# Spreading the next batch's first scans: the pace table of a two-stream recurrent kernel

## The reference, cut to what matters

```
x : (16, 512, 128)
xn = layernorm(x)
s  = selective_scan(xn, forward) + reverse(selective_scan(reverse(xn), backward))   # 2 x 16 states
g  = mixture_ffn(xn)          # router top-2 factor * (gelu(xn w1 + b1) w2 + b2)
x  = x + s * silu(g)                                   # "block A"
xn = layernorm(x)
s  = mamba2_like(xn)          # conv of 4 taps, chunked state recurrence, gated norm
g  = 2 layers of [ local attention over windows of 64 (8 heads of 64) ; gated ffn 128 -> 341 -> 128 ]
x  = x + s * silu(g)                                   # "block B"

selective_scan(x):  delta = softplus(low_rank(x));  h_t = exp(delta_t A) h_{t-1} + delta_t B_t x_t
                    y_t = sum over 16 states of C_t h_t + D x_t
```

## Time and profile before

| | |
|---|---|
| median of 3 runs | 4148.99 us (4142.99 to 4150.77) |
| profiled execution | 4157.49 us, span 4155.7 us |
| PE busy | 3285.2 us, 79% |
| ACT busy | 2603.5 us, 63% |
| DVE busy | 2552.8 us, 61% |
| POOL busy | 1726.6 us, 42% |
| mean granted TensorE clock | 0.905 of full speed |
| chain that ended last | PE 45%, DVE 20%, ACT 13%, issue 12%, POOL 9% |
| DMA engines | mean 5 GB/s, all but idle after the first slice |

### The profile page before, as it was taken

The page is one execution under the profiler, slowest core; times in us unless marked ns, Lnnn a source line. Parts: engine busy times, 40 slices in busy tenths (PEclk is TensorE's granted clock), DMA queues, the critical chain, the costliest instruction groups (busy, mean ns, idle before and its releaser), DMA issues.

```text
span 4155.7 us, 57708 instructions
## 1 busy us (share of the span) xinstructions
PE 3285.2 (79%) x17248; PEld 1929.7 (46%) x17248; DVE 2552.8 (61%) x4239; ACT 2603.5 (63%) x5871; POOL 1726.6 (42%) x1428
## 2 busy tenths in 40 slices
PE   4688878877788878887887788787887887888787
PEld 2354444544444444444544445445444544455443
DVE  5575766657556565666647666575666656666443
ACT  4466667665676656667666676656767566676554
POOL 2353343524435353343533535344353533535332
PEclk9798999999999999998989999989999899989898
DMA  2000000000000000000000000000000000000000
GB/s 83 3 1 1 6 1 6 1 1 7 1 7 1 1 7 1 7 1 1 6 1 7 1 7 1 1 7 1 7 1 1 7 1 7 1 1 3 1 3 3
DMA packets 18444, 21.03 MB, mean 5 GB/s; under 512 B 769, under 2 KB 17153, under 8 KB 17793
## 3 DMA queue, kind: packets, MB, share of 16 engines
q1 hardware_dynamic: 18048, 16.44, 1.2%
HBM read 12.24 MB, written 4.19 MB: 4 GB/s over the span
## 4 chain that ended last, share of the span: by engine, by line
PE 45%; DVE 20%; ACT 13%; issue 12%; POOL 9%; DMA 0%; DVEq 0%; POOLq 0%; ACTq 0%; SPq 0%
PE bank L564 8%; PE bank L626 5%; POOL hc L1464 4%; PE bank L813 3%; DVE tmp L1375 3%; DVE hst L1235 3%; PE bank L797 3%; PE bank L746 3%; POOL Pm L1537 2%; PE bank L547 2%; PE bank L532 2%; PE bank L773 2%; DVE tmp L1370 2%; DVE bank L1227 2%; PE bank L756 2%
## 5 line engine op out<-in xcount | busy, mean ns | idle before, releaser
L1464 POOL TENSOR_TENSOR hc<-hst,Cs 128x512 f32<-128x512 f32 x512 | 655.4, 1280 | 967.5 <-DVE hst L1235 957.2
L1235 DVE TENSOR_TENSOR_SCAN hst<-dA,bank 128x512 f32<-128x512 f32 x512 | 625.0, 1221 | 133.5 <-issue 58.9
L564 PE MATMUL bank<-W,xs 128*128 128x512 f32 x960 | 493.7, 660 | 25.5 <-DVE tmp L1375 23.8
L1537 POOL TENSOR_TENSOR Pm<-Pm,rinv 128x512 f32<-128x512 f32 x256 | 271.5, 1060 | 455.8 <-DVE rinv L1395 438.5
L927 ACT COPY Cs<-bank 128x512 f32<-128x512 f32 x512 | 299.3, 585 | 247.2 <-PE bank L547 217.4
L1227 DVE TENSOR_TENSOR bank<-u,bank 128x512 f32<-128x512 f32 x512 | 351.3, 686 | 158.7 <-PE bank L547 154.6
L547 PE MATMUL bank<-parts,sel 96*128 96x512 bf16 x1024 | 356.9, 423 | 107.8 <-DVE hst L1235 42.0
L1522 POOL TENSOR_TENSOR oT<-tmp 128x512 f32<-128x512 f32 x256 | 325.0, 1269 | 247.0 <-DVE tmp L1375 184.3
L921 ACT ACTIVATE dA<-delta,neg_a 128x512 f32<-128x512 f32 x512 | 372.6, 728 | 67.8 <-DVE hst L1235 67.1
L532 PE MATMUL bank<-C,hc 128*128 128x128 f32 x2048 | 353.6, 302 | 35.5 <-POOL hc L1464 35.5
L1054 ACT ACTIVATE Pm<-bank,mx 128x128 f32<-128x128 f32 x1024 | 366.7, 387 | 16.3 <-DVE mx L1389 14.7
(11 more groups left out here) (224 smaller groups left out, 6197.0 us busy)
## 6 DMA issues: line engine op xcount, KB each, us to landing
W<-wpack SPq DMA_DIRECT2D x1, 4498.0 KB, 13.3
x_tok<-x SPq DMA_DIRECT2D x16, 256.0 KB, 2.9
out<-xa SPq DMA_DIRECT2D x16, 256.0 KB, 2.2
rot<-tables SPq DMA_DIRECT2D x2, 512.0 KB, 15.9
wc_f<-taps SPq DMA_DIRECT2D x1, 1024.0 KB, 19.2
C<-cpack SPq DMA_DIRECT2D x1, 721.0 KB, 14.5
Pm<-mask SPq DMA_DIRECT2D x1, 320.0 KB, 14.8
tmp<-rowpack SPq DMA_DIRECT2D x1, 256.0 KB, 17.1
```

Of the source, the lines that this page charges most:

```text
L564: mm(b[:, :], weights, rhs, start=True, stop=True).then_inc(full(ring, job), 1)
L1235: v.tensor_tensor_scan(o, a, b, 0.0, ALU.mult, ALU.add).then_inc(sem("a_h"), 1)
L1464: g_.tensor_tensor(hc[:, k % 2, :], hst[:, k % 2, :], Cs[:, k % 2, :], ALU.mult)\
L1537: g_.tensor_tensor(windows, windows, over(rinv[:, k % 2, :], P), ALU.mult).then_inc(sem("t_P"), 1)
```

## The change

The table's entry that let P8 end with layer 1's fifteenth slot (B slot 46) is moved to B slot 42. The prologue's nine A slots are so run over the seven B slots from 35 on, for eleven before, and the ten scan slots are interpolated from B slot 42 to the last, for from B slot 46.

```diff
-PACE = [(0, 1), (LAYER, 10), (LAYER + UNITS_END, A_END), (LAYER + LAYER_SLOTS, HEAD + 5), (LAYER + LAYER_SLOTS + 4, PRO),
-        (LAYER + LAYER_SLOTS + UNITS_END, SCAN1), (B_SLOTS, A_SLOTS)]
+PACE = [(0, 1), (LAYER, 10), (LAYER + UNITS_END, A_END), (LAYER + LAYER_SLOTS, HEAD + 5), (LAYER + LAYER_SLOTS + 4, PRO), (LAYER + LAYER_SLOTS + 11, SCAN1),
+        (B_SLOTS, A_SLOTS)]
```

## The result

The changed kernel takes 4176.3 us (median of 4 runs, 4174.9 to 4182.8) against 4149.3 us for the kernel before on the same chip (4143.0 to 4150.8): ratio 1.0073, 95% interval 1.0057 to 1.0090. It is 27 us slower; 17 were predicted. The profiled execution has a span of 4181.0 us at a mean granted clock of 0.897 (before: 4155.7 us, 0.905).

What follows compares the result with a forecast made beforehand. No engine is busy over four fifths of the span, so the fit of five in-order queues was taken as the bound. 6.6 - 0.5 - 4.9 = +1.2 us a step, 14 steps, +17 us: 4166 us, range 4110 to 4205.

Steps and rivals of the forecast that it cites:

- Tail, -4.9: From the last feed-forward matmul to the next step's first: two DVE scans fewer, 4.9 us gained, bounds 3.8 and 5.6.
- the Silu and x2 pair: ACT's Silu and DVE's two x2 operations in the tail: if they set it, it stays above 12 us.
- Attention part, +6.6: Layer 1's first attention unit to its output projection: 5.8 us more on ACT plus 0.8 on PE, bounds 3.5 and 9.5.
- The two waits that the replay named: Behind DVE's delta block: PE waits about 3 us for POOL's Pm of unit 5, ACT 1.4 us at the gate.
- The gate block: P8's Silu table load, gate and load back on ACT, now ahead of the projection: 3.2 us.
- Three scans ahead of the projection: Two scans of 1.3 us on ACT before the last copies, and scan 2 on PE, some 0.8 us.
- The order of the prologue with the delta block: P0 to P4 earlier fill idle time; waits at the gate and first Gelu give it back: left out of the sum.
- Feed-forward, -0.5: From layer 1's projection to its last feed-forward matmul: one scan in slot 48 for two, 0.5 us gained, bounds 0 and 1.3.
- PE sets the pace: Rival, slots 38 to 42: PE never waits for the delta block, attention part grows only 3.5 us; 4122 us, chance 0.30.
- Half clock: Rival, attention part: matmuls behind PE's holes run at 1.2 GHz, 3 us more a step; 4208 us, chance 0.12.
- the holes it named: Two PE waits in the replayed attention part, 2183.3 to 86.5 and 87.8 to 91.0; half clock was expected behind the second.
- The two ends cancel: Rival: the tail gives what the attention part takes, within 0.5 us; 4149 us, chance 0.16.

Runs made afterwards that it cites:

- e1: Changed kernel's compressed prologue (B slots 35 to 41), with the ten scans left where the kernel before has them (slots 46 to 52): 4203.9 us, 1.0133.
- e7: e1 with the gate's Silu and its table loads on ACT moved to B slot 46, behind the attention part: 4170.4 us, 1.0058.
- e3: Changed kernel with the gate's Silu and its two table loads on ACT moved from slot 41 to 46, behind the last oT copy: 4112.7 us, 0.9911.
- e5: Changed kernel with 13 and 10 matmuls that nobody reads ahead of the transposes of layer 1's units 5 and 6: 4178.0 us, 1.0077.
- e8: Changed kernel with 6 and 6 unread matmuls on PE in the tail, ahead of scans 8 and 9: 4156.3 us, 1.0012.
- e11: Kernel before with the same 6 and 6 unread matmuls in the tail as e8: 4150.8 us, 1.0004.
- e6: e3 with DVE's delta block also cut in two around unit 6's maximum, unit 5's reciprocal and fo: 4167.0 us, 1.0045.
- e9: e3 with P0 to P8 one each in slots 35 to 43 and the ten scans over slots 44 to 52: 4149.5 us, 0.9996.
- e12: e10 with 8 more unread matmuls ahead of layer 0's transpose of unit 7: 4103.1 us, 0.9889.
- e10: e3 with the 6 and 6 unread matmuls in the tail of e8: 4090.1 us, 0.9856.

## Why the prediction was right, and where it was short

Direction, mechanism and the cancellation of two large terms were right: 81 us lost in the attention part, 65 won in the tail over fourteen steps (92 and 69 predicted). The 10 us by which the sum missed are a net figure, and that it is so small is in part luck. The attention part took 11 us less than forecast, the tail gave 3 less, and the feed-forward and the stretch behind the tail took 10 and 11 more; inside the attention part three wrong prices came out within 0.7 us a step of their sum. By its own steps:

- *Tail, -4.9.* -4.9 measured over the loop steps (13.5 predicted from L821's end to L1308, 13.6 measured). Scans on DVE set it, and the Silu and x2 pair did not take their place.
- *Attention part, +6.6.* +5.9 by the table's cuts, 5.7 from the first score matmul to L797. The two waits that the replay named came out within 0.1 us, their places didn't: the delta block starts 28.0 us behind the first score matmul (30.4 predicted), the transpose of unit 5 38.4 (41.0), L797 50.3 (51.8). It was replayed on a step whose first half was 2.4 us longer than that of most steps, by half clock. Its split was off too. The gate block: 3.2 predicted, 2.7 (e1 against e7) or 2.4 (after against e3). Three scans ahead of the projection: 2.6 + 0.8 = 3.4 predicted, 1.4 (after against e1) or 1.7 (e3 against e7) measured; this is the mis-sized term, as ACT had idle time between its copies for part of them: from unit 7's maximum to L797 it is idle for 2.7 us of 10.4 in e1 and 1.9 of 11.9 in after (means of eleven steps). The order of the prologue with the delta block: nothing on balance predicted ("I let it stand"), 1.8 measured (e7 against before). 1.8 + 2.7 + 1.4 = 5.9.
- *Feed-forward, -0.5.* +0.2. One scan fewer stands there, but 2.2 us of half clock a step do too, for none before; in e3, and in the four steps of after that have no half clock there, it is 16.1, that is -0.8; with 3.4 us of it, 17.8.
- *What the sum left out.* This is where it fell short. The sum ended at the next L1308 and took everything behind it as unchanged. The stretch behind took 1.6 us more in a loop step (+11 us over fourteen) with 4.9 us more half clock. With the feed-forward's +10 against its forecast and the tail's +3, less the attention part's 11 and layer 0's 2, these make the prediction's 17 into the fourteen steps' 28; the medians differ by 27, the two profiled executions as a whole by 25.

The rivals: *PE sets the pace* fell; the projection comes 5.7 us later in the mean (5.15 in the pair of steps shown), not 3.5, and PE waits 3.23 us at the place where this rival had it not wait. *Half clock* named a real effect at the wrong place: the half clock rose by 7.7 us a step, but behind the holes it named it cost at most about 1.3 us (e5), for 3 in the rival. The larger cost shows behind the tail, and keeping PE at work in the tail takes 20 to 25 us back (e8, with e11 as the control). *The two ends cancel* fell by 1.2 us a step in the three parts that it is about (+5.9, +0.2 and -4.9), and by the cost behind them. e8, without most of that cost, is at 1.0012, near no change.

The Trainium skill ("ScalarE: Activation LUTs", What ACT_TABLE_LOAD costs) puts a drain of about 1.38 us beside each load; an estimate by that page is 3.2 + 2.8 = 6.0 us for the gate block with its two switches. Moving the block gave 2.7 and 2.4 us, less than even its rows' 3.2, and its rows after show loads of 1.28 us and nothing beside them but the wait for `fo`. The measurement decides: no such drain is in this kernel.

Open: why the half clock falls where it does. e6 and e9 each moved work out of one place and got more half clock at another; e3 has a short stretch behind the tail (77.8) without any filler, so the longer one of after isn't the short tail's doing alone. And e5 bounds the price of half clock in the attention part, but doesn't give it. The share of the delta block in the prologue's 1.8 us is open too.

## What to carry to other kernels

Price a moved block by what stands behind it on its in-order engine: the same gate of 3.2 us, the same work in all, is worth 2.4 to 2.7 us a step on one or the other side of the last copy that the critical matmul waits for, and moving it turned a loss of 0.7% into a gain of 0.9%, about half of that by this stretch. Spreading independent work into idle time pays (here the tail) only after what it displaces has been cleared from the full stretch. Where a stretch with a waiting PE is cut short, follow the granted clock into the stretch behind it, and try throwaway matmuls there if that one is bound by PE and has more half clock than before. Read more than one step before a replay: here the step chosen was 2.4 us off the usual one in the very part that mattered. And look at every stretch after adding instructions, as e12's did what they were meant to and lost more at the loop's turn.

## What the runs showed of the hardware

- Half clock is cheaper than it looks: before, 43.5 of 251.7 us a step run at 1.2 GHz. Among the eleven steps of one kernel, whose instructions are the same, a stretch grew by 0.32 us (behind the tail), 0.39 us (layer 0), 0.27 us (attention part) and 0.44 us (feed-forward) for each us of half clock in it, and the tail by nothing (0.03). These are fits over the fourteen traces, each step taken against its own kernel's mean; the correlations are 0.91 to 0.97, the tail's 0.13. They are no bound on what fillers bring: e5 took 7.9 us out of the attention part and gained nothing.
- With identical instructions, steps of the loop aren't equally long: many lie near 249.2, 252.6 and 256.0 us within one execution (e5's, of the fourteen, all within 0.4 us of the last two), and the clock's low stretches lie differently in them. A mean over steps is needed to see terms of 1 us.
- Twelve matmuls of 512 columns that nobody reads, 2.9 us of PE a step, made a kernel of 4113 us 23 us faster and one of 4176 us 20 us faster, and left one of 4150 us unmoved.
- Eight more in another place came with a stall of PE of 2.60 us at the loop's turn with nothing to wait for, where e10 had 0.79.
